# Second attention of a four-layer gated stack: where ScalarE weighs the gathered expert rows, and in which order GpSimd does its turn

## The reference, cut to what matters

```python
# layer 0, feed-forward: the two chosen experts' rows, weighed and added
selected = expert_out[topk_idx, tok]
x = x + tanh(g_ffn[0]) * sum(selected * topk_weights[..., None], axis=1)
# layer 1, attention: 8 heads of 16, queries and keys run along the 256 channels
n = layernorm(x)                                # by token, 256 channels
qh = n.reshape(B, 8, 16, 256); kh = vh = ctx.reshape(B, 8, 16, 256)
qk = einsum('bhdq,bhdl->bhql', qh, kh) * 0.25
ret = einsum('bhql,bhdl->bhdq', softmax(qk), vh).reshape(B, 128, 256)
x = x + tanh(g_xattn[1]) * gamma * ret
```

## Time and profile before

| | |
|---|---|
| time, median of 3 runs | 1425.56 (1424.91 to 1430.61) |
| time of the profiled execution | 1424.39 |
| its span | 1422.6 |
| TensorE busy, share of the span | 82% |
| VectorE, ScalarE, GpSimd busy | 63%, 38%, 31% |
| mean granted TensorE clock | 0.922 of full |
| stage 2 in the trace | about 409 to 647 |

### The profile page before, as it was taken

How to read it: one execution, slowest core, us unless ns; L and a number is a source line. 1 busy time by engine, 2 the same in 40 slices (tenths; PEclk the granted TensorE clock), 3 DMA queues, 4 the chain that set the end, 5 groups by cost and what they waited for, 6 DMA issues and landing times.

```text
span 1422.6 us, 34438 instructions
## 1 busy us (share of the span) xinstructions
PE 1161.7 (82%) x12364; PEld 905.7 (64%) x12364; DVE 902.3 (63%) x2468; ACT 534.2 (38%) x1013; POOL 437.9 (31%) x943
## 2 busy tenths in 40 slices
PE   4989889966846767787899799998566699999998
PEld 2667667645733333445666566676354599999998
DVE  3556657655555566776666577778566566666665
ACT  2546446644533444562010233232215433333332
POOL 2445555648857556521100111113122100000000
PEclk8899999987975878898999899999789899999999
DMA  5332333215763233321000100000105300000000
GB/s 180 106 105 76 120 120 127 93 38 171 216 184 97 86 98 94 100 85 60 1 0 0 31 23 19 17 22 7 37 0 152 107 1 1 16 0 15 0 15 16
DMA packets 91469, 93.86 MB, mean 66 GB/s; under 512 B 10276, under 2 KB 83380, under 8 KB 90588
## 3 DMA queue, kind: packets, MB, share of 16 engines
q1 hardware_dynamic: 85500, 78.24, 17.5%
q0 software_dynamic: 4992, 13.66, 3.2%
q10 hardware_dynamic: 864, 0.43, 0.1%
HBM read 56.76 MB, written 35.53 MB: 65 GB/s over the span
## 4 chain that ended last, share of the span: by engine, by line
PE 40%; DVE 12%; issue 10%; POOL 4%; ACT 3%; DVEq 1%; DMA 1%; POOLq 0%; ACTq 0%; SPq 0%
PE psum L2329 5%; PE psum L1387 4%; PE psum L1389 4%; PE psum L1388 4%; PE psum L2084 3%; PE psum L1405 2%; PE psum L1407 2%; PE psum L1406 2%; PE psum L2069 1%; DVE mx L2221 1%; PE psum L2376 1%; PE psum L1750 1%; POOL rstd L687 1%; PE psum L1752 1%; PE psum L1751 1%
## 5 line engine op out<-in xcount | busy, mean ns | idle before, releaser
L685 POOL TENSOR_SCALAR veps<-mv 128x1 f32<-128x1 f32 x112 | 26.7, 239 | 680.6 <-DVE mv L1255 367.3
L1387 PE MATMUL psum<-xnTh,w7h 128*128 128x256 f32 x512 | 146.9, 287 | 0.0
L1389 PE MATMUL psum<-xnTh,w7l 128*128 128x256 f32 x512 | 145.6, 284 | 0.0
L1388 PE MATMUL psum<-xnTl,w7h 128*128 128x256 f32 x512 | 145.6, 284 | 0.0
L782 DVE TENSOR_REDUCE mx<-psum 128x6 f32<-128x960 f32 (+3 forms) x80 | 80.7, 1009 | 69.4 <-PE psum L980 68.3
L1464 ACT ACTIVATE sil<-psum 128x256 f32<-128x256 f32 x128 | 49.3, 385 | 189.2 <-PE psum L1389 189.2
L1487 DVE TENSOR_TENSOR hTf<-sil,psum 128x256 f32<-128x256 f32 x128 | 53.9, 421 | 97.5 <-ACT sil L1464 97.5
L1989 DVE TENSOR_REDUCE mx<-psum 128x4 f32<-128x1024 f32 x64 | 77.2, 1208 | 50.3 <-PE psum L2058 50.3
L2084 PE MATMUL psum<-PT,arena 128*32 128x256 f32 x1024 | 82.5, 444 | 23.5 <-POOL arena L1945 23.4
L1389 PEld LDWEIGHTS psum<-xnTh,w7l 128*128 128x128 f32 x512 | 99.0, 193 | 0.0
L1387 PEld LDWEIGHTS psum<-xnTh,w7h 128*128 128x128 f32 x512 | 98.7, 193 | 0.0
(11 more groups left out here) (359 smaller groups left out, 3229.5 us busy)
## 6 DMA issues: line engine op xcount, KB each, us to landing
xs<-qpad SPq DMA_DIRECT2D x17, 1024.0 KB, 5.0
ctxT<-in_ctxT SPq DMA_DIRECT2D x48, 128.0 KB, 2.2
ext<-qscr SPq DMA_DIRECT2D x96, 64.0 KB, 2.4
w_raw<-in_w SPq DMA_DIRECT2D x16, 384.0 KB, 3.3
arena<-in_w SPq DMA_DIRECT2D x4, 1280.0 KB, 10.1
PT<-xs SPq DMA_DIRECT2D x39, 128.0 KB, 2.7
ys<-yt SPq DMA_DIRECT2D x39, 128.0 KB, 2.7
q_parts<-kscr SPq DMA_DIRECT2D x66, 64.0 KB, 2.2
```

The source lines that it names most:

```text
L1387: MM(o, wh, xnTh[:, s, c], start=(c == 0), stop=False)
L1388: MM(o, wh, xnTl[:, s, c], start=False, stop=False)
L1389: t = MM(o, wl, xnTh[:, s, c], start=False, stop=(c == NC - 1))
```

## The change

Two lists of instructions in stage 2 are put in another order. No instruction is added or taken away.

ScalarE: the weighing of tile i+4 at the end of turn i goes away; the weighing of tile i+5 comes into turn i, between the second and the third exponential of tile i-1 (or in front of the copies in turns that have no exponentials).

GpSimd: the turn becomes lay of i, sum_rows of i+4, gather of i+6, then rs and normalise of i+3, add of i-2, operands of i+3. At the very start the gather of tile 2 is issued ahead of rs of tile 0, that of tile 3 behind it; rs of tile 1 stands ahead of its sum and gather.

```diff
             def body(i, s):
                 pp, b, n = i - 2, i, i + 3
+                def fetch_rows():
+                    if 2 <= n + 1 < NB:
+                        sum_rows(pool, n + 1)
+                    if inside(n + 3):
+                        gather(pool, n + 3)
+                if n == 0:
+                    gather(pool, 2)
+                if inside(b):
+                    lay(b, s)
+                if n >= 2:
+                    fetch_rows()
                 if inside(n):
                     rs(n, 1 - s)
                     if n >= 2:
                         normalise(P, pool, n, 1 - s)
+                    else:
+                        fetch_rows()
                 if inside(pp):
                     add(pp)
-                if inside(n):
-                    if n >= 2:
-                        operands(P, pool, n, 1 - s)
-                    if 2 <= n + 1 < NB:
-                        sum_rows(pool, n + 1)
-                    for m in (2, 3) if n == 0 else (n + 3,):
-                        if m < NB:
-                            gather(pool, m)
-                if inside(b):
-                    lay(b, s)
+                if inside(n) and n >= 2:
+                    operands(P, pool, n, 1 - s)
...
                     for k in range(4):
                         act.wait_ge(F("st").sem, F("st").at(p, k + 1))
                         nc.scalar.activation(PT[:, 1024 * k:1024 * (k + 1)], bank(6, 2), ACT.Exp, scale=0.25).then_inc(F("p").sem, 1)
+                        if k == 1 and inside(i + 5):
+                            weigh(act, i + 5)
+                elif inside(i + 5):
+                    weigh(act, i + 5)
...
                         nc.scalar.copy(qop[96:120, b % 3].rearrange("p (m e) n -> p m e n", e=2)[:, :, e], src).then_inc(F("mxT").sem, 1)
-                if 2 <= i + 4 < NB:
-                    weigh(act, i + 4)
```

## The result

The changed kernel takes 1375.62 (median of 4, 1374.32 to 1376.56), the kernel before, run beside it on the same chip, 1426.22 (1424.91 to 1430.61). The ratio is 0.9639 [0.9617, 0.9662]: 3.6% or 50.6 less. Predicted were 1371 and 3.7% less.

The account below looks back on a forecast made before the run. The prediction took stage 2's full turn of 14.7 to be bound by a ring of waits, not a full engine. Savings of 45.1, 3.6, 2.0 and 2.5 made 53.2, taking 1424.4 to 1371, range 1361 to 1391.

Parts of the forecast that it names:

- start, to the first copies: Stage 2's start: rs of tile 0 later, +0.9; VectorE's wait for tile 3's sum gone, -2.9; together -2.0.
- second turn: The turn after the start, 14.7 before: put midway between 14.7 and 9.7, at 12.2, so -2.5.
- nine full turns: Stage 2's turns with all work: from 14.7 each to 9.7 each, -45.1 in all.
- two turns without gathers: Stage 2's turns with sums but no gathers, 11.7 and 11.3 before: priced at 9.7 each, -3.6.
- The ring: Full turn of stage 2: no engine fills its 14.7; each waits for a step the next has put last.
- The weighing: ScalarE in stage 2: fits the 0.96 idle ahead of the third exponential, gap left 0.1; cost 0, gather wait 0.
- The signs: Expected stage 2 profile: full turns 9.5 to 9.8, VectorE idle under 0.5 a turn, granted clock 0.95 or more.
- signs of being wrong: Stage 2: weighing waiting for a gather, scores waiting for the queries' load, or values still taking 1.94 each turn.
- What bounds next: Full turn after the change: VectorE at 9.5, including 0.35 for its split beside busy GpSimd; taken as 9.7.
- the rival that gave it one cold quarter a turn: TensorE's clock falls in each turn of stage 2, costing up to 1.6 a turn: 1389; chance 0.10.
- the slower one: TensorE stays at 1.2 GHz through stage 2, turns of 15.4 with waits: 1455; chance 0.03.
- The rival of contention: GpSimd's and VectorE's work in stage 2 stretch each other until a turn takes 11: 1387; chance 0.08.

Follow-up runs that it names:

- e1: Changed kernel with GpSimd's turn and the start back in the old order, only ScalarE's new weighing place kept: 1385.93, ratio 0.9713 against the kernel before.
- e2: Kernel before with only GpSimd's new order; ScalarE still weighs tile i+4 at the end of its turn: 1407.57, ratio 0.9861 against the kernel before.
- e3: Changed kernel with tile i+5 weighed behind the copies, at the end of ScalarE's turn, not between exponentials: 1380.48, ratio 0.968 against the kernel before.
- e11: Kernel before with GpSimd's new order, but its add moved between lay and the sum: 1393.87, ratio 0.9765 against the kernel before.
- e4: Changed kernel with TensorE's scores 1 of the next tile issued ahead of values 3: 1373.29, ratio 0.9624 against the kernel before.
- e5: Changed kernel with an unread copy of 128 x 256 added to GpSimd's lay: 1373.26, ratio 0.9612 against the kernel before.
- e6: Changed kernel with unread statistics of 128 x 256 added to VectorE for each tile: 1384.56, ratio 0.9701 against the kernel before.
- e8: Changed kernel with two unread GpSimd instructions added in each of turns 10 to 12, which have no gathers: 1377.31, ratio 0.9644 against the kernel before.
- e9: Changed kernel with GpSimd's add put ahead of rs from turn 10 on, no work added: 1371.63, ratio 0.9616 against the kernel before.

## Why the prediction was right, and where its terms were off

The spans differ by 50.1; the sum gave 53.2. The waits that the change was to end are gone, so the mechanism held; that the stage's total came within 0.7 of the sum is in part luck, since the full turns gave 2.2 more and the three smaller terms together some 1.5 less. Term by term, in the order of the working:

| term | predicted | in the profile |
|---|---|---|
| start, to the first copies | -2.0 | -1.5 (28.43 to 26.95 behind the first gather) |
| second turn | -2.5 | -2.1 (14.63 to 12.56) |
| nine full turns | -45.1 | -47.3 (132.4 to 85.1) |
| two turns without gathers | -3.6 | -3.1 (22.95 to 19.89) |
| sum | -53.2 | -53.9 |
| the stages around this one | 0 | +2.3 ahead of the first gather, +1.5 behind |

**The ring.** That a full turn was a ring of waits, opened by weighing earlier and by summing and laying first, is what e1, e2, e3 and e11 bear out. Both halves are needed: ScalarE's alone is worth 41.5, GpSimd's alone 19.9, together some 51. These don't add: each alone takes away part of the same ring. ScalarE's alone meets late gathers; GpSimd's alone keeps the late weighing.

**The weighing.** A gap of 0.1 was to be left ahead of the third exponential; 0.17 was. The gathers cost nothing in the full turns, as priced. That this price depends on GpSimd's order, e1 showed; I had not counted it as such in its expectation.

**GpSimd's order.** One unbroken row, as said, of 9.39 instead of 9.48. The one DMA step that I called tight, the queries' load, is waited for only at the very start.

**The signs.** Three of those that I named did not come out as written. Full turns of 9.39 lie under the 9.5 to 9.8. VectorE is idle 0.93 a turn by its busy time (85.14 less 76.80, over nine), not under 0.5; its one longer wait is the 0.52 ahead of the second maximum. The granted clock is 1.00 in the full turns, but 0.91 over the stage from 411 to 593, since it takes in the start. By the letter two signs of being wrong were there as well: the weighing waited for gathers four times, and scores once for the queries' load. Both lie ahead of the full turns, and both were there before the change too (twice and once); the sign should have named the full turns.

**What bounds next.** I took 9.7 from VectorE's 9.5 and some lateness. The turn is 9.39. The mis-sized piece is the split beside a busy GpSimd: 0.35 in the sum, but in the full turns its last piece takes 271 ns and L703 229 on average, against 175 unhindered, 0.15 together. With this in place of 0.35 the sum gives 9.30, and 0.09 is left for the lateness. The average of 525 belonged to the phase of the old order, in which GpSimd's two-input work stood beside the split; in the new one GpSimd is in rs and the normalising then. And e4, e5 and e6 show that VectorE does not bound alone: GpSimd's row and the line of ScalarE with TensorE end within 0.2.

**The turns without gathers** I priced at 9.7 too; they take 9.94, for the same contention at another phase: 0.66 for an operation of 0.17.

**The clock.** 2.4 GHz in all full turns, as taken; the rival that gave it one cold quarter a turn, and the slower one, have nothing in the profile. In the second turn it is 0.65, and that turn came out at 12.56 beside the 12.2 put midway.

**The median.** 1375.6 against 1371: the stage gave 0.7 more than the sum. The rest lies outside it, and 1.3 of it is that the profiled execution, 1374.32, lies under the median. The first gather comes 2.3 later, and between the profiles of this study that point lies up to 8.4 apart, though no kernel changes anything ahead of it; the chain that leads there in the changed kernel holds four transfers (PT<-xs) of 2.2 to 3.7. Whether these move the point, no run here shows. The later stages took 1.5 more. The change touches neither.

The rival of contention was right in kind and wrong in size: it acts, but the split's excess is 0.15 in the full turns and some 0.6 in the three without gathers, and not 1.3. What stays open: whether the later stages' 1.5 is more than scatter (788.08 before, 789.57 and 787.70 in two profiles of the same changed kernel), and what the line of 9.43 in e4 consists of in detail.

## What to carry to other kernels

When an engine shows long waits that name no releaser, follow the last work that the waiting instruction reads, in the timeline: here a small operation (0.9) placed last in its engine's turn, though its data had long been there, closed a ring over three engines, and with the late sum and values it cost 5.3 a turn, TensorE's lower clock among it. Moving a step earlier shortens the ring only as far as every other step in it has slack: ask of the transfer that feeds it (e1) and of the buffer that its engine's other work frees (e2). Once several engines are full to within 0.2, their phase decides: the price of two engines' contention, measured in one order, does not carry over to the next.

## What the runs showed of the hardware

- A small VectorE operation on SBUF that starts just behind a two-input operation of GpSimd on 128 x 256 ends about when that one does, 0.03 behind it in the changed kernel. For 128 x 16 with two inputs: 0.66 instead of 0.17, beside GpSimd's L703 (the changed kernel, e6) and beside its add (e8). A cast with one input is held too. In the timeline of e2_gpsimd_only:
```profile
502.94 0.67 POOL L709 TENSOR_TENSOR xparts<-xres,xparts 128x256 bf16<-128x256 f32 x1
502.96 0.68 DVE L701 CAST mxp<-mx 128x16 bf16<-128x16 f32 x1
```
- GpSimd's operation need not have two inputs: its casts hold VectorE as well, 0.39 instead of 0.17 with an end 0.02 behind the cast's. In the timeline of the kernel before:
```profile
552.12 0.40 POOL L707 CAST xparts<-xres 128x256 bf16<-128x256 f32 x1 [0.17 <-POOL xres L703]
552.15 0.39 DVE L703 TENSOR_TENSOR mxr<-mx,mxp 128x16 f32<-128x16 f32 x1
```
- The normalising (L1916, 1.24 long) did not hold it to its end: in the full turn shown above VectorE's L709, started 0.32 behind it, took 0.25. A phase in which the split stands beside the normalising is therefore a cheap one.
- It goes the other way too: when VectorE's combine was there first (500.33, 0.41 long), GpSimd's L709, started 0.09 behind it, took 0.85 instead of 0.67.
- With it, 0.43 of added work cost 0.88 of time (e6), 0.34 cost 0.15 (e5), and GpSimd left idle for 3.11 made a turn 0.6 shorter (e9).
